# A last attention layer with its norms on ScalarE, and expert products merged to 512 columns

## The chip, the cores and the metric

One NeuronCore of a Trainium2 chip runs the whole program: TensorE (PE) multiplies, VectorE (DVE) and ScalarE (ACT) work on rows in SBUF and PSUM, GpSimd (POOL) on rows in SBUF only and issues indirect DMAs, and SyncE (SP) issues most DMAs. The metric is the device time of one execution in microseconds; lower is better.

## What is computed

Four transformer layers over 32 row blocks of 128 rows and 256 columns. Layers 0 and 1 are cross-attentions with a feed-forward net behind layer 0, layer 2 is a decoder layer (causal attention, cross-attention, then a mixture of 8 experts of which each row takes 2), layer 3 is a windowed attention with a gate, an RMS norm and a centring over each block. The code numbers the attentions 0 to 4, so that "layer 4" there is the last one. The parts which the change touches:

```
router_weights = softmax(xf @ rw + rb);  topw, topi = top_k(router_weights, 2);  topw = softmax(topw)
h   = gelu(xf @ w1[e] + b1[e]);  eo = h @ w2[e] + b2[e]          # for each expert e
x   = layernorm(x + sum over the row's 2 experts of topw * eo)   # ln3
attn = (softmax(q k / 4, window of 128) v) @ Wo + bo             # 16 heads, one key/value head
gate = silu(concat(attn, query) @ Wg + bg)
out  = attn * gate + query * (1 - gate)
x_hat = out * rsqrt(mean(out^2) + 1e-6) * rms_w
y    = x_hat - mean(x_hat over the 128 rows of a block)
```

## The kernel before

Every engine has a program of its own, and semaphores order them. It has three stages.

**Attention stage.** `slots` runs 8 iterations of 16 slots (4 attentions for 4 row blocks) and a tail. In the last attention's slots the router's logits are made; seven slots later `rank` (L956) counts, with a triangular and an all-ones matmul in float32 over `ohm5`, how many rows before each row chose the same expert. DVE turns ranks into positions (`ranks`, `positions`), and POOL scatters each row twice into `sorted_x` (`scatter`, L1949), where every expert has a span of its own; `base` keeps each expert's next free row.

**Hand-over and experts.** After the last ranks DVE makes tables (`tlink`, L1717, one linked step after another): `tails`, from which SP zeroes 128 rows behind each expert's last; the number of tiles of each expert; for each of 71 tiles its address and expert (loop at L1733, three steps an expert); then the positions in the packed result (L1757 to L1760). SP loads tile 0 after all zero fills, scatters and tables (L591 to L606). For each tile PE runs `up` (16 products 128x128, L1071), the transposes of the next tile (L685) and `down` (L1075). For `down` the hidden values and the weights are split into a high and a low part, and high x high, high x low and low x high are summed in `ps_w`, in matmuls of 256 columns (L1084). DVE splits the hidden values (`tile_split`, L1779) and adds the bias to the result (`tile_y`, L1773), POOL splits the weights of expert e while e-1 runs (`split_w2`, L2010), ACT applies gelu and copies the weights of `up`.

**Last layer.** `cslots` runs 32 slots (one for each row block) and a drain. Names with c(d) are the row block d slots ahead. POOL gathers the two expert rows of block c(4) (`gather`, L2036), DVE combines them for c(3) (`combine`, L1826: two products, then the statistics), POOL takes the root (`c_root`), DVE applies the norm for c(2) (`combine_apply`, L1841), POOL makes the residual rows (`c_residual`, L2047). PE runs scores, transposed scores and the products with the values for now and c(-1), then the gate for c(-2) (L1118, L1122); DVE takes the maxima of the scores (`maxima`, L1482), which PE transposes (L877) before the transposed scores, and applies the gate (`gate_open`, `gate_apply`). The RMS norm of c(-3) goes over ACT (`mean_square`), POOL (L2086), DVE (`rms_apply`, L1866), PE (`mean`, L1129) and ACT (`finish`, L1370), which copies the result for the store of c(-4). Before the first slot come constants (L1135 to L1148 on PE, L1809 to L1824 on DVE): products of the biases with weights that let bo, bv and bg be added once.

Each engine carries out its program in the written order; nothing is reordered, so what stands ahead of a waiting operation on its engine, and what behind, can be read from the code.

## Time and profile before

| | us |
|---|---|
| median of 3 runs | 2302.21 |
| lowest, highest | 2299.98, 2303.04 |
| the profiled execution | 2305.83 |
| its span, first to last instruction | 2304.0 |
| attention stage, to about | 1380 |
| experts, from 1407 to about | 1900 |
| last layer, maxima of block 0 and of block 31 | 1923.6, 2276.1 |

The profile is one execution. PE was busy 92% of the span, DVE 71%, ACT 47%, POOL 45%; the granted TensorE clock had a mean of 0.976 of full speed. These shares are means over three stages with different limits. In a timeline row stand the start and duration in microseconds, engine, line, operation, output<-input with the number of operations merged, and in brackets how long the engine had been idle and what ended that. A row of a group has the busy time in microseconds, the mean of one in nanoseconds, and the idle time before.

### The profile page before, as it was taken

Reading aid. Unit: us, or ns where it says so; the run is one execution under the profiler, and the core shown is the slowest. Engines: PE = TensorE matmul, PEld = TensorE weight load, DVE = VectorE, ACT = ScalarE, POOL = GpSimd, SP = SyncE. Lnnn points to the kernel's source line nnn. Section 1 sums busy time; section 2 is a strip of 40 time slices with the busy share of each in tenths; the row PEclk is TensorE's granted clock in tenths of the full one; section 3 lists DMA queues with packets and bytes.
Section 4 is the critical chain, followed back from the end, with each engine's and each line's share of the span. In section 5 each row is a group of like instructions: output and inputs, shape, how many; then the busy total and the mean of one; then the engine's idle time right before and its main releaser. Section 6 shows DMA issues by size and latency. Waiting matters only on the chain.

```text
span 2304.0 us, 84589 instructions
## 1 busy us (share of the span) xinstructions
PE 2108.5 (92%) x31768; PEld 1837.1 (80%) x31769; DVE 1644.6 (71%) x3373; ACT 1092.9 (47%) x2804; POOL 1038.3 (45%) x1304
## 2 busy tenths in 40 slices
PE   5999999999999999999999975999999997888897
PEld 4877877878878878878878755999999996676776
DVE  4688787787787887887887875444544446889986
ACT  2345344354454344453444433556555553555554
POOL 3445455455455454554554634110211007767763
PEclk9999999999999999999999987999999997999989
DMA  8401001001001001001000103121221112211110
GB/s 196 163 3 38 8 21 43 7 19 42 9 19 39 11 19 36 16 19 31 18 22 4 39 29 133 50 64 39 60 70 39 39 32 82 59 55 56 56 50 21
DMA packets 93477, 101.02 MB, mean 44 GB/s; under 512 B 23968, under 2 KB 84384, under 8 KB 93088
## 3 DMA queue, kind: packets, MB, share of 16 engines
q1 hardware_dynamic: 84128, 72.02, 10.4%
q0 software_dynamic: 8704, 25.19, 3.5%
q8 instruction: 203, 3.33, 0.6%
q14 instruction: 58, 0.48, 0.1%
q10 hardware_dynamic: 384, 0.01, 0.0%
HBM read 64.94 MB, written 32.24 MB: 42 GB/s over the span
## 4 chain that ended last, share of the span: by engine, by line
PE 56%; issue 17%; DVE 15%; ACT 5%; POOL 4%; DVEq 1%; SPq 1%; DMA 1%; POOLq 0%; ACTq 0%
PE ps_scores L1071 10%; PE ps_w L1084 9%; PE ps_o L897 8%; PE ps_scores L858 4%; ACT pt_all L1242 4%; PE ps_qk L779 4%; PE ps_qk L745 4%; DVE rs L1492 3%; PE ps_xv L685 2%; PE ps_xv L763 2%; DVE lower L1473 2%; PE ps_scores L805 1%; PE ps_scores L865 1%; PE ps_w L944 1%; POOL rstd L1940 1%
## 5 line engine op out<-in xcount | busy, mean ns | idle before, releaser
L1485 DVE TENSOR_REDUCE mb<-ps_scores 128x16 bf16<-128x2048 f32 x160 | 365.8, 2286 | 57.8 <-PE ps_scores L838 54.2
L1492 DVE RECIPROCAL rs<-ps_o 128x256 f32<-128x256 f32 x160 | 280.4, 1752 | 33.1 <-PE ps_o L897 29.0
L1242 ACT ACTIVATE pt_all<-ps_scores 128x512 f32<-128x512 f32 x512 | 263.5, 602 | 48.4 <-PE ps_scores L865 48.4
L1071 PE MATMUL ps_scores<-tiles,w_now 128*128 128x128 f32 x2272 | 267.4, 276 | 1.2 <-DVE tiles L1767 1.2
L1071 PEld LDWEIGHTS ps_scores<-tiles,w_now 128*128 128x128 f32 x2272 | 262.0, 193 | 1.8 <-issue 1.8
L1328 ACT ACTIVATE tiles<-ps_scores,b1s 128x128 f32<-128x128 f32 x568 | 154.2, 383 | 204.6 <-PE ps_scores L1071 178.8
L1940 POOL TENSOR_TENSOR rstd<-ve,neghalf 128x1 f32<-128x1 f32 x192 | 109.6, 571 | 308.0 <-DVE ve L1503 268.1
L1084 PE MATMUL ps_w<-w_split,g_split 128*128 x1704 | 224.3, 288 | 7.5 <-DVE g_split L1787 5.8
L1924 POOL TENSOR_TENSOR lower<-lower,consts 128x512 fp32r<-128x512 f32 x160 | 171.3, 1071 | 123.7 <-DVE lower L1473 77.5
L1084 PEld LDWEIGHTS ps_w<-w_split,g_split 128*128 128x128 f32 x1704 | 210.0, 192 | 12.4 <-issue 9.5
L1917 POOL TENSOR_TENSOR qbd_all<-qT,consts 128x512 fp32r<-128x512 f32 x160 | 167.3, 1046 | 104.9 <-ACT kT L1228 74.4
L897 PE MATMUL ps_o<-pt_all,vz 128*32 128x128 f32 x5120 | 176.4, 277 | 2.3 <-issue 2.3
L897 PE MATMUL ps_o<-pt_all,onz 128*32 128x128 f32 x5120 | 171.2, 273 | 0.0
L1777 DVE TENSOR_TENSOR tiles<-ps_w,tiles 128x256 f32<-128x256 f32 x71 | 30.2, 425 | 193.6 <-PE ps_w L1084 193.6
L897 PEld LDWEIGHTS ps_o<-pt_all,vz 128*32 128x32 f32 x5120 | 131.7, 110 | 26.3 <-issue 17.6
L1320 ACT COPY w_now<-w_experts 128x2048 f32 x72 | 140.1, 1948 | 25.1 <-DVE pos_all L1760 25.1
L1945 POOL TENSOR_TENSOR xr<-xn,arena 128x256 f32<-128x256 f32 x128 | 93.1, 727 | 124.1 <-DVE xn L1507 124.1
L1213 ACT ACTIVATE xT<-ps_xv,cols_all 128x128 f32<-128x128 f32 x256 | 103.2, 453 | 90.1 <-PE ps_xv L685 87.0
L897 PEld LDWEIGHTS ps_o<-pt_all,onz 128*32 128x32 f32 x5120 | 144.6, 110 | 0.2
L2018 POOL CAST w_split<-w_raw 128x512 fp32r<-128x512 f32 x32 | 18.2, 609 | 276.8 <-DVE g_split L1787 271.5
L1231 ACT ACTIVATE qT<-ps_qk,cols_all 128x128 fp32r<-128x128 f32 x192 | 60.4, 369 | 173.2 <-PE ps_qk L779 173.2
L2041 POOL DMA_INDIRECT arena<-sorted_y,pidx x64 | 63.2, 987 | 173.5 <-ACT pidx L1354 158.5
(247 smaller groups left out, 4830.2 us busy)
## 6 DMA issues: line engine op xcount, KB each, us to landing
tiles<-sorted_x SPq DMA_DIRECT2D x72, 128.0 KB, 2.0
sorted_y<-tiles SPq DMA_DIRECT2D x71, 128.0 KB, 1.7
w_experts<-in_L_xattn_e_w SPq DMA_DIRECT2D x8, 1024.0 KB, 10.4
w_raw<-in_L_xattn_e_w POOLq DMA_DIRECT2D x8, 1024.0 KB
ct_scratch<-cT SPq DMA_DIRECT2D x32, 128.0 KB, 1.7
x_scratch<-x2b_all SPq DMA_DIRECT2D x32, 128.0 KB, 1.7
arena<-x_scratch SPq DMA_DIRECT2D x32, 128.0 KB
cT<-ct_scratch SPq DMA_DIRECT2D x32, 128.0 KB, 2.1
```

The costliest lines, as they stand in the source:

```text
L897: last = mm(ps_o[32 * q:32 * q + 32, 2 * kind + c, :], w, pt[:, SLOTS * q + PAIR * c + par, :], start=par == 0, stop=par == 1, tile_positi ...
L1071: last = mm(ps_s[:, 2 * par + j // 4, P * (j % 4):P * (j % 4 + 1)], w1_now[:, par, c, P * j:P * (j + 1)], xgT[par][:, c, :], start=c == 0, ...
L1084: last = mm(ps_w[:, 0:D], g_split[:, g_, j, :].bitcast(F32R), w2_split[:, bass.ds(odd * (2 * FC * D) + (w_ * FC + j) * D, D)].bitcast(F32R ...
L1213: last = nc.scalar.activation(xT[n["s"]][:, c, :], src[:, c, :], ACT.Identity, bias=col[b_][:, c:c + 1], scale=col[g][:, c:c + 1])
L1242: nc.scalar.activation(pt[:, 4 * g:4 * g + 4, :].rearrange("p h q -> p (h q)"), ps_s[:, g, :], ACT.Exp, bias=bias, scale=LAYER[l]["scale"] ...
L1320: nc.scalar.copy(w1_now[:, par].rearrange("p c n -> p (c n)"), w1f[:, bass.ds(e * (KC * FF), KC * FF)]).then_inc(w1_copied, 1)
L1328: last = nc.scalar.activation(gT[:, j, :], ps_s[:, 2 * par + j // 4, P * (j % 4):P * (j % 4 + 1)], ACT.Gelu, bias=b1s[par][:, j:j + 1])
L1485: V.tensor_reduce(mb[:].rearrange("p (g r) -> p g r", g=BANKS)[:, :, 0:SLOTS], ps_s[:].rearrange("p g (h k) -> p g h k", h=SLOTS), AX_X, A ...
L1492: V.reciprocal(rs[:], ps_o[:, 2:4, :]).then_inc(recip_ready, 1)
L1917: G.tensor_tensor(qbd[p].bitcast(F32R), qT[:].unsqueeze(2).to_broadcast([P, KC, PAIR, P]), hmask.unsqueeze(1).unsqueeze(3).to_broadcast([P ...
L1924: G.tensor_tensor(qbd_lo.bitcast(F32R), qT_lo.unsqueeze(2).to_broadcast([P, KC, PAIR, P]), hmask.unsqueeze(1).unsqueeze(3).to_broadcast([P ...
L1940: G.tensor_tensor(rstd[kind][:], ve[kind][:], neghalf[:], ALU.pow).then_inc(done, 1)
```

## The change

It has four parts.

1. *Last layer.* The combination's norm is applied by ACT, as yb x rstd + c_nb with c_nb = -mean x rstd from POOL, and the RMS scaling by ACT too; the RMS weight moves behind the centring, into DVE's `finish`, which reads PSUM and replaces ACT's copy. `finish` stands ahead of the maxima. DVE's combination of c(3) and gate of c(-2) are written in turns instead of one after the other. On POOL the gather moves to the end of the slot, the low part of the queries (`expand_lo`) from the end to its beginning.
2. *Constants ahead.* The bias products of the last layer are made on PE and DVE while the experts' first tile is awaited; so is the window mask. The first slot's work is reordered: keys and values before the transposes, scores of block 0 before the projections of block 1.
3. *Hand-over to the experts.* The per-tile tables are made for all 8 experts in one operation each (`past`, `steps`, 128x568), 12 linked steps instead of 41. The tails are zeroed half an iteration earlier, 640 rows for each expert instead of 128. The update of the positions comes after the copies of tiles 0 and 1. The ranks are counted in bfloat16.
4. *Experts.* High and low weights lie side by side, so that the high hidden part multiplies both in one matmul of 512 columns; the sum of the two halves is a second DVE operation in `tile_y`. `tile_split` has one cast and one subtraction of 1024 columns instead of two each of 512. POOL's split has 8 casts of 256 and 16 subtractions of 128 columns instead of 4 of 512 and 8 of 256.

```diff
@@ rank (PE)
-            mm(ps_w[:, D:D + (NS + 1) * E], tri, ohm5[:].rearrange("p s e -> p (s e)"), start=True, stop=False)
+            mm(ps_w[:, D:D + (NS + 1) * E], tri_b, ohm5[:].rearrange("p s e -> p (s e)"), start=True, stop=False)
@@ SP, in the last iteration's slots; POOL waits for tail_zeroed before its last scatters
+            if last and tau == TPI // 2:
+                sp.wait_ge(consts_ready, 1)
+                sp.wait_ge(tails_ready, 1)
+                for e in range(E):
+                    r = sp.value_load(tails[0:1, e:e + 1], min_val=0, max_val=DUMMY - TAIL)
+                    sp.dma_start(sorted_x[bass.ds(r, TAIL), :].rearrange("(a p) d -> p a d", p=P),
+                                 zeros[:].unsqueeze(1).to_broadcast([P, TAIL // P, D])).then_inc(tail_zeroed, 16)
@@ tables (DVE)
-        for e in range(E):
-            tlink(V.tensor_scalar(tb[:, 4], tile_iota, incl[:, e:e + 1], None, ALU.is_ge))
-            tlink(V.tensor_tensor(eid, eid, tb[:, 4], ALU.add))
-            tlink(V.scalar_tensor_tensor(ex_, tb[:, 4], n_t[:, e:e + 1], ex_, ALU.mult, ALU.add))
...
+        tlink(V.tensor_tensor(past[:], tile_iota.unsqueeze(2).to_broadcast([P, TILES, E]), by_tile(incl), ALU.is_ge))
+        tlink(V.tensor_tensor(steps[:], past[:], by_tile(shift[:]), ALU.mult))
+        V.tensor_reduce(eid, past[:], AX_X, ALU.add)
+        tlink(V.tensor_reduce(row_, steps[:], AX_X, ALU.add))
@@ down (PE)
+            def part(g_, j):
+                n = 2 * D if g_ == 0 else D
+                return mm(ps_w[:, 0:n], g_split[:, g_, j, :].bitcast(F32R),
+                          w2_split[:, bass.ds(odd * (2 * FC * D) + j * 2 * D, n)].bitcast(F32R),
+                          start=j == 0 and g_ == 0, stop=j == FC - 1 and g_ == 0)
@@ tile_y (DVE)
-            V.tensor_tensor(ys[par], ps_w[:, 0:D], b2.rearrange("p e d -> p (e d)")[:, bass.ds(e * D, D)], ALU.add).then_inc(b_y, 1)
+            V.tensor_tensor(ys[par], ps_w[:, 0:D], b2.rearrange("p e d -> p (e d)")[:, bass.ds(e * D, D)], ALU.add).then_inc(b_part, 1)
+            wait_apart(dve, b_part, k + 1)
+            V.tensor_tensor(ys[par], ps_w[:, D:2 * D], ys[par], ALU.add).then_inc(b_y, 1)
@@ last layer (ACT), combine_apply before mean_square, rms_apply after xt_evac
+            nc.scalar.activation(xn[n["s"]][:], yb[n["p"]][:], ACT.Identity, bias=c_nb[:], scale=rstd[2][:]).then_inc(c_xn, 1)
...
+            nc.scalar.activation(xh[n["p"]], go, ACT.Identity, bias=0.0, scale=rstd[3][:]).then_inc(c_xh, 1)
@@ c_root (POOL)
+            root(2, c_ln, COMBINE * b + 5, c_root_done)
+            wait(pool, c_root_done, b + 1)
+            G.tensor_tensor(c_nb[:], c_nm[:], rstd[2][:], ALU.mult).then_inc(c_rstd, 1)
@@ finish (DVE), ahead of maxima
+            wait(dve, c_mean, b + 1)
+            wait(dve, c_at, last_at)
+            wait(dve, c_out[n["p"]], 16 * n["h"])
+            V.tensor_tensor(fin[n["p"]], ps_w[:, D:2 * D], row3["L3_xattn_rms_w"][:], ALU.mult).then_inc(c_fin, 1)
```

Of the moved instructions three places are shown, each first before, then after. Numbers of lines are those of the file they stand in. First PE, one tile's down product: address loads and its first matmuls.

```order
L1078 ISA x2
L98 REGISTER_ALU
L1084 ISA
L1084 MATMUL ps_w<-w_split,g_split 128x256
L1084 ISA
L1084 MATMUL ps_w<-w_split,g_split 128x256 x2
```

```order
L1110 ISA x2
L99 REGISTER_ALU
L1116 ISA
L1116 MATMUL ps_w<-w_split,g_split 128x512
L1116 MATMUL ps_w<-w_split,g_split 128x256
```

Of three matmuls of 256 columns for each of the 8 blocks, one of 512 and one of 256 are left. Next DVE, one slot of the last layer from behind the maxima (the gate is L1855, L1861, L1863, L1864 before and L1888, L1893, L1898, L1902 after; the combination is L1831 to L1839 and L1865 to L1884).

```order
L1845 TENSOR_SCALAR xn<-yb,mv,rstd 128x256
L1492 RECIPROCAL rs<-ps_o 128x256
L1494 TENSOR_TENSOR oT<-ps_o,rs 128x256
L1855 TENSOR_TENSOR arena<-ps_w,row_L_xattn_bg 128x256
L1869 SCALAR_TENSOR_TENSOR arena<-arena,rstd,row_L_xattn_rms_w 128x256
L1831 SCALAR_TENSOR_TENSOR arena<-arena,w_all 128x256
L1833 SCALAR_TENSOR_TENSOR yb<-arena,w_all 128x256
L1835 BN_STATS st_2<-yb 128x6
L1837 BN_AGGR mv<-st_2 128x2
L1839 TENSOR_SCALAR ve<-mv 128x1
L1861 SCALAR_TENSOR_TENSOR arena<-arena 128x256
L1863 SCALAR_TENSOR_TENSOR arena<-arena 128x256
```

```order
L1532 RECIPROCAL rs<-ps_o 128x256
L1534 TENSOR_TENSOR oT<-ps_o,rs 128x256
L1888 TENSOR_TENSOR arena<-ps_w,row_L_xattn_bg 128x256
L1865 SCALAR_TENSOR_TENSOR arena<-arena,w_all 128x256
L1893 SCALAR_TENSOR_TENSOR arena<-arena 128x256
L1871 SCALAR_TENSOR_TENSOR yb<-arena,w_all 128x256
L1898 SCALAR_TENSOR_TENSOR arena<-arena 128x256
L1875 BN_STATS st_2<-yb 128x6
L1902 TENSOR_TENSOR arena<-arena,xr 128x256
L1880 BN_AGGR mv<-st_2 128x2
L1883 TENSOR_SCALAR c_nm<-mv 128x1
L1884 TENSOR_SCALAR ve<-mv 128x1
```

The norm and the RMS scaling are gone from DVE, and each operation now has one of the other chain between it and its predecessor. Last POOL, one slot of the last layer (L2041 and L2093 are the gathers).

```order
L1940 TENSOR_TENSOR rstd<-ve,neghalf 128x1
L1917 TENSOR_TENSOR qbd_all<-qT,consts 128x512
L2041 DMA arena<-sorted_y,pidx 128x256 x2
L2086 TENSOR_TENSOR rstd<-ve,neghalf 128x1
L2059 TENSOR_TENSOR arena<-arena 128x256
L2051 TENSOR_TENSOR xr<-xn,row_L_xattn_ln_g 128x256
L2053 TENSOR_TENSOR arena<-xr,arena 128x256
L2054 TENSOR_TENSOR xr<-xr,row_L_xattn_ln_b 128x256
L1924 TENSOR_TENSOR lower<-lower,consts 128x512
```

```order
L1990 TENSOR_TENSOR rstd<-ve,neghalf 128x1
L2102 TENSOR_TENSOR c_nb<-c_nm,rstd 128x1
L1974 TENSOR_TENSOR lower<-lower,consts 128x512
L1967 TENSOR_TENSOR qbd_all<-qT,consts 128x512
L2144 TENSOR_TENSOR rstd<-ve,neghalf 128x1
L2108 TENSOR_TENSOR xr<-xn,row_L_xattn_ln_g 128x256
L2110 TENSOR_TENSOR arena<-xr,arena 128x256
L2111 TENSOR_TENSOR xr<-xr,row_L_xattn_ln_b 128x256
L2116 TENSOR_TENSOR arena<-arena 128x256
L2093 DMA arena<-sorted_y,pidx 128x256 x2
```

The low part of the queries moved from the end to the third place, the gathers to the end, the difference (L2059, L2116) behind the residual rows, and c_nb is new.

## Rows read from the trace of the kernel before

**Rows 1.** Busy time of each engine in three stretches, with TensorE's granted clock.

```profile
1300.00:1450.00 150.00, 107.63 (x1551) 95.63 (x1552) 98.96 (x239) 59.29 (x136) 61.94 (x80) 0.84 0.23 78
1600.00:1700.00 100.00, 98.34 (x842) 97.07 (x841) 47.12 (x102) 57.00 (x133) 19.94 (x26) 1.00 0.19 59
2000.00:2100.00 100.00, 86.80 (x1568) 71.19 (x1569) 88.12 (x142) 52.12 (x158) 70.58 (x87) 0.95 0.19 55
```

**Rows 2.** All instructions of line 1485: number, min/median/max ns, first and last start.

```profile
L1485 DVE TENSOR_REDUCE mb<-ps_scores x32: 2291/2292/2293, 1923.6 to 2276.1; 128x16 bf16<-128x2048 f32 x32
```

**Rows 3.** Timeline, start and duration: two maxima that follow each other near the end.

```profile
2257.08 2.29 DVE L1485 TENSOR_REDUCE mb<-ps_scores 128x16 bf16<-128x2048 f32 x1
2267.26 2.29 DVE L1485 TENSOR_REDUCE mb<-ps_scores 128x16 bf16<-128x2048 f32 x1 [1.42 <-PE ps_scores L838]
```

**Rows 4.** Groups by line and shape, 1950 to 2280: busy us, mean ns, idle.

```profile
L1831 DVE SCALAR_TENSOR_TENSOR arena<-arena,w_all 128x256 f32<-128x256 f32 x26 | 26.1, 1004 | 0.0
L1869 DVE SCALAR_TENSOR_TENSOR arena<-arena,rstd,row_L_xattn_rms_w 128x256 f32<-128x256 f32 x28 | 23.2, 830 | 3.4
L1864 DVE TENSOR_TENSOR arena<-arena,xr 128x256 f32<-128x256 f32 x29 | 19.4, 668 | 1.0
L1845 DVE TENSOR_SCALAR xn<-yb,mv,rstd 128x256 f32<-128x256 f32 x27 | 11.7, 435 | 0.0
L1855 DVE TENSOR_TENSOR arena<-ps_w,row_L_xattn_bg 128x256 f32<-128x256 f32 x28 | 11.6, 415 | 0.0
L1940 POOL TENSOR_TENSOR rstd<-ve,neghalf 128x1 f32<-128x1 f32 x27 | 18.0, 666 | 37.0 <-DVE ve L1839 36.9
```

**Rows 5.** Timeline: the same VectorE product beside two different GpSimd operations.

```profile
1910.56 0.96 POOL L2041 DMA_INDIRECT arena<-sorted_y,pidx  x1 [0.30 <-issue]
1910.95 0.48 DVE L1831 SCALAR_TENSOR_TENSOR arena<-arena,w_all 128x256 f32<-128x256 f32 x1 [5.09 <-DMA arena<-sorted_y,pidx]
...
2065.30 1.22 POOL L1924 TENSOR_TENSOR lower<-lower,consts 128x512 fp32r<-128x512 f32 x1
2065.55 1.26 DVE L1831 SCALAR_TENSOR_TENSOR arena<-arena,w_all 128x256 f32<-128x256 f32 x1
```

**Rows 6.** Chain that ended last: an expert tile, and four of line 910's.

```profile
1481.49 3.57 PE ps_scores L1071 x32
1485.28 2.96 PE ps_w L1084 x24
...
1984.85 0.86 PE ps_w L910 x4
```

**Rows 7.** Timeline of the experts, DVE casts without and beside GpSimd's split.

```profile
1605.40 0.75 DVE L1784 CAST g_split<-tiles 128x512 fp32r<-128x512 f32 x2
1612.24 1.50 DVE L1784 CAST g_split<-tiles 128x512 fp32r<-128x512 f32 x2
```

**Rows 8.** Timeline of the hand-over to the experts.

```profile
1378.02 1.85 PE L962 MATMUL ps_w<-route_all,one_f 128*128 128x32 f32 x8
...
1390.21 0.96 POOL L1953 DMA_INDIRECT sorted_x<-x2b_all,posu  x1 [0.30 <-issue]
...
1393.01 5.98 DVE L1741 TENSOR_SCALAR tbi<-xT 128x71 int32<-128x71 f32 x1
...
1401.06 0.36 SPq L600 DMA_DIRECT2D tiles<-sorted_x  x1
1401.09 0.26 DVE L1759 TENSOR_SCALAR yb<-yb,shift 128x64 f32<-128x64 f32 x1
```

**Rows 9.** Timeline of the hand-over to the last layer.

```profile
1899.96 0.42 DVE L1777 TENSOR_TENSOR tiles<-ps_w,tiles 128x256 f32<-128x256 f32 x1 [5.01 <-PE ps_w L1084]
...
1905.61 0.29 ACT L1354 CAST pidx<-pos_all 128x2 uint32<-128x2 f32 x2 [13.99 <-DVE row_L_xattn_bg L1821]
1906.68 1.03 POOL L2041 DMA_INDIRECT arena<-sorted_y,pidx  x1 [158.46 <-ACT pidx L1354]
```

**Rows 10.** The page's DMA issues: KB each, median us from issue to landing.

```profile
sorted_y<-tiles SPq DMA_DIRECT2D x71, 128.0 KB, 1.7
```

328 lines of the change are left out of this document (176 added, 152 removed).

## The prediction

> **What bounds the kernel now.** I read the busy time by stretch first; it tells three regimes apart [rows 1]: among the experts (1600 to 1700) TensorE (PE) is busy 98.3 of 100 us and VectorE (DVE) 47; in the last layer (2000 to 2100) DVE has 88.1, PE 86.8 at a granted clock of 0.95; the stretch of the hand-over to the experts (1300 to 1450) has gaps on all engines, and a clock of 0.84. So a microsecond taken from PE among the experts counts in full, one taken from DVE in the last layer counts until PE is the bound, and in between the chain decides.
>
> The last layer's maxima (L1485) run 32 times, from 1923.6 to 2276.1 [rows 2]: 352.5 us over 31 steps, 11.37 us a slot. What a slot costs when DVE is not late is seen near the end, where gathers and combination have run out: from 2257.08 to 2267.26, 10.18 us, and there DVE waited 1.42 us for PE [rows 3]. That is the floor which PE sets; 1.19 us a slot lies above it.
>
> **The last layer.** Part of that excess is DVE work that lasts longer than it needs. The first combination product (L1831) has a mean of 1004 ns, the RMS scaling (L1869) 830, the gate's sum (L1864) 668, though a like one on 128x256 that reads PSUM takes 415 (L1855) [rows 4]. The timeline shows with whom they collide: L1831 lasts 1.26 us beside GpSimd's (POOL's) L1924, but 0.48 beside POOL's gather L2041 [rows 5]. The change removes from DVE the normalisation L1845 (0.435) and the RMS scaling (0.830), adds the weighted finish (like L1855, 0.415) and one tiny scaling c_nm (taken at 0.15), and puts the gather last on POOL, where the combination and gate operations of DVE run beside it. With L1831 at its undisturbed 0.48 and L1864 at the 0.42 of L1855, DVE loses 0.435 + 0.830 + 0.52 + 0.25 - 0.415 - 0.15 = 1.47 us of work a slot. It had 88.1/100 x 11.37 = 10.0, so about 8.5 remain. That is under the floor of 10.18: PE sets the slot. Writing the two chains in turns also hides their waits on each other; I don't add that, as DVE has slack already.
>
> The norm's new price is latency. The bias c_nb is one more POOL operation of 128x1, at most the 666 ns of L1940 [rows 4], and the application on ScalarE (ACT) waits for it with mean square and maxima copy queued behind. ACT is busy 52 of 100 us [rows 1] and has room for two more operations of the size of L1855. POOL, with 70.6 per 100 us (8.0 a slot) plus at most 0.7, stays under 10. On DVE the finish now stands ahead of the maxima, waits for ACT's copy of the attention rows, and PE's next transposes wait for those maxima. In the undisturbed slot nothing stood there, so I charge its issue step, 0.3 us of the 0.415, in full: a slot of 10.45 instead of 11.37 us (the last two, short already, lengthen a little: that is inside the rounding). 31 x 0.92 = **28.5 us**. Bounds: 10.2 gives 36, 11.0 gives 11.
>
> The Trainium skill, "SBUF — State Buffer", who interferes with whom, calls the pair of ports that VectorE and GpSimd share an exclusive lock, taken by a VectorE operation with two SBUF inputs against GpSimd operations that read SBUF, the second fully blocked. The pair of L1831 rows agrees. By that rule the new order would save what I count, and the casts in the expert stage, which may take both ports, would block in the same way; that is the rival on the other side below.
>
> **The experts.** Each of the 71 tiles has 24 matmuls of 256 columns, 2.96 us, after 3.57 us of up projections (L1071) [rows 6]: 2.96/24 = 0.123 us each. The change makes them 8 of 512 and 8 of 256 columns; the columns streamed are the same, 8 of 24 starts go. If all cost lies in the columns, the gain is zero. If a 256-column one costs 0.123 and a 512-column one its stream alone, take L910: its four instructions of one 128x256 product in float32, at two passes, need 0.86 us, 0.215 each [rows 6], and that is the same stream as 512 columns at one pass. Then 8 x (0.215 + 0.123) = 2.70, 0.26 less. I take 0.18, between this and a fixed cost for each start (0.123 less 256/512 of 0.215 is 0.016, of which eight go: 0.13). 71 x 0.18 = 12.8 us, bounds 0 and 18.
>
> Against it stands a longer DVE chain before each down product: the tile's sum becomes two operations (0.42 each), while two casts and two subtractions become one each. I reckon 0.6 us more, which the 3.57 us of up projection still hide. Where POOL splits the next expert's weights the cover is gone: two casts (L1784) take 1.50 instead of 0.75 us [rows 7]. POOL's split now has 24 short operations instead of 12, so it lasts longer, perhaps 2 tiles instead of 1 for each of 6 experts; at 0.4 us for each of 12 tiles: minus 5 us. Net **8 us**, bounds -5 and 18.
>
> The Trainium skill, "TensorE: Matmul & The Clock Gate", back-to-back issue gap, gives N/2.4 + 2.5 ns, 109 ns at 256 columns. The row says 123, so here it doesn't hold as it stands; by it the merge would save only 8 x 2.5 ns a tile, 1.4 us in all, which is the second rival.
>
> **The hand-over to the experts.** Before, the ranks' float32 matmuls (L960, L962; the last takes 1.85 us from 1378.02), then 41 linked table steps on DVE, one of which, L1741, lasted 5.98 us beside POOL's split; tile 0 is loaded at 1401.06. The last scatter starts at 1390.21 and takes 0.96 us [rows 8]. After, the ranks are in bfloat16 (1.5 us earlier) and the table has 12 steps; from about 1380, at even 0.6 us each, it ends by 1388. So the scatter is late next: 1391.17 - 1.5 + its landing, for which I take a tile store's 1.7 us [rows 10] = 1391.4. The load comes 9.7 us earlier. SyncE (SP) has given its zero fills off by then: they are issued half an iteration before, five times as long (8 x 640 rows), and only POOL's last scatters wait for them. Given back: the 15 position updates of 0.26 us (L1759) now stand between tile 1's copy and tile 0's split, 4 us of which ACT's gelu covers about half: 2 us. Net **8 us**, bounds 4 and 10. In the seven earlier iterations the ranks' ten matmuls lie on PE's queue at full clock; half precision and half the passes save perhaps 0.4 us each, **3 us**, bounds 0 and 7.
>
> **The hand-over to the last layer.** ACT's index copy started at 1905.61, after waiting 13.99 us for the constants (L1821) [rows 9]. With the constants made ahead, the gather waits only for the last tile's store: that can be issued from 1900.4 on, when DVE's last sum ends [rows 9], lands 1.7 us later [rows 10], and comes 1 us later for the longer chain: with some 0.3 us of issue 1903.4, against 1906.7 for the gather [rows 9]. **3 us**, bounds 0 and 5; the earlier scores of row block 0 are swallowed by the third block's combination, which stands ahead of its maxima.
>
> **The sum.** 28.5 + 8 + 8 + 3 + 3 = 50.5 us. The profiled execution took 2305.83 us, 1.83 outside its span, and is 3.6 above the median of 2302.21. So 2255.3 by its own time, and 2251.7 by the median: 2252.
>
> **Rivals.**
> *The slot stays with DVE or POOL.* POOL's residual operations and the difference now come together before the gather; if they reach into DVE's five operations with two SBUF inputs, each may go to 1.26 us as L1831 did. Two of five add 1.6 us to 8.5 and give 10.1, three 10.9. Slot 11.0: 28.5 becomes 11.5, total 33.5, 2269. For it: DVE's 88% and POOL's 71%; against it: the 0.48 beside the gather.
> *The merge saves nothing on PE* (all cost in the columns, or 2.5 ns a start) while the longer split costs 5 us: experts +4 instead of -8, 2264. For it: no row has a 512-column full-array product. Both together: 2281.
> *Slower than before: the single cast starves.* L1741 waited through the whole of POOL's split. If the one cast of 1024 columns, or the subtraction behind it, does so each time, PE waits for about the split's length, some 12 us, six times: 72 us against 50.5, 2324. It decides from 8.4 us an expert. Against it: today's casts only double beside the same operations [rows 7], and they get in between.
> *The change doesn't act*: the slot was never DVE's. Then the 1.42 us wait for PE in the undisturbed slot would stand in all slots; it stands only where the work is gone [rows 3], so this has next to no weight.
>
> **How the numbers follow.** Forecast 0.52, slot rival 0.20, merge rival 0.15, both 0.07, slower 0.04, near nothing 0.02. The forecast's own bounds run from 2232 (slot at the floor, merge at its best) to 2262; the range goes on over the two single rivals to 2276 and leaves out the double and the slow one. Faster by more than 0.2% (4.6 us, about what a measurement of this kernel can tell from no change): 0.93; within it: 0.02; slower: 0.05.
>
> **What would show it.** Right: the maxima 10.2 to 10.7 us apart with DVE waiting for PE's scores, the combination product near 0.48 us, tiles 6.5 to 6.6 us apart, the first tile load near 1388 (3 us of the ranks included), the first gather 3 us after the last store's issue. Wrong: combination or gate operations still above 0.8 us, PE waiting for maxima or for the ScalarE norm, down products still 2.9 us, PE stalls of several us wherever POOL splits weights, or a granted clock well under 0.95 in the last layer.

## The result, and the profile after

The changed kernel took 2282.89 us in the median of five executions (2274.13 to 2288.45), the kernel before 2302.21 (2299.98 to 2306.12): a ratio of 0.990, with a 95% interval of 0.988 to 0.992. It is faster, by 19 us; 50 were forecast, and 2282.89 lies above the range of 2232 to 2276.

By stages, from one profile each (the changed kernel's is of its fastest execution, 2274.13 us; the last column is another execution of the same file, on another chip, and belongs to the experiments):

| | forecast | measured | the same file on a second chip |
|---|---|---|---|
| to the first tile's sum (hand-over, ranks) | -11 | -10.5 | -9.7 |
| first to last tile's sum | -8 | -14.8 | -14.8 |
| last tile's sum to the first maxima | -3 | -3.3 | -3.4 |
| 31 slots of the last layer | -28.5 | -2.4 | -38.8 |
| drain | 0 | -0.7 | -0.7 |
| span | -50.5 | -31.7 | -67.4 |

The first sum is DVE's L1777 or L1820 of tile 0. The two spans differ by more than the two medians, 31.7 against 19.3 us: the profiled execution of before is 3.6 us above its median, that of the changed kernel 8.8 below. Two terms are near, the experts gave more, and the last layer gave next to nothing. The maxima of the last layer, which answer [rows 2], first in the changed kernel:

```profile
L1525 DVE TENSOR_REDUCE mb<-ps_scores x32: 2280/2281/2293, 1895.0 to 2245.1; 128x16 bf16<-128x2048 f32 x32
```

350.1 us over 31 steps, 11.29 a slot (before: 11.37), most of them 11.6. Busy time by stretch, as [rows 1]:

```profile
1300.00:1450.00 150.00, 120.64 (x1577) 104.58 (x1571) 94.91 (x221) 66.38 (x154) 68.61 (x104) 0.89 0.23 75
1600.00:1700.00 100.00, 100.00 (x754) 94.23 (x755) 49.37 (x92) 60.12 (x138) 24.17 (x51) 1.00 0.20 60
2000.00:2100.00 100.00, 86.27 (x1619) 70.07 (x1622) 72.54 (x150) 58.74 (x174) 74.46 (x96) 1.00 0.19 58
```

In the last layer DVE fell from 88.1 to 72.5 of 100 us, 8.4 us in a slot of 11.6, where 8.5 were forecast. But PE didn't become busier: no engine is full. The groups by form (as [rows 4]) show the operations as quick as hoped:

```profile
L1865 DVE SCALAR_TENSOR_TENSOR arena<-arena,w_all 128x256 f32<-128x256 f32 x22 | 10.5, 476 | 0.0
L1902 DVE TENSOR_TENSOR arena<-arena,xr 128x256 f32<-128x256 f32 x22 | 9.0, 407 | 0.0
L1910 DVE TENSOR_TENSOR arena<-ps_w,row_L_xattn_rms_w 128x256 f32<-128x256 f32 x22 | 9.3, 425 | 58.1 <-ACT arena L1427 31.2 <-issue 25.7 <-PE ps_w L1169 1.3
```

The freed time is now idle time ahead of L1910, the weighted finish: 58.1 us in 22 slots. The timeline of one slot says what it waits for:

```profile
2048.04 0.40 PE L882 MATMUL ps_scores<-mT,ecol_b 32*128 32x128 bf16 x16
2048.12 1.24 POOL L2093 DMA_INDIRECT arena<-sorted_y,pidx  x1 [0.16 <-issue]
2048.24 0.41 ACT L1447 ACTIVATE arena<-arena 128x256 f32<-128x256 f32 x1
2049.66 1.13 POOL L2093 DMA_INDIRECT arena<-sorted_y,pidx  x1 [0.30 <-issue]
2051.06 2.06 ACT L1269 ACTIVATE pt_all<-ps_scores 128x512 f32<-128x512 f32 x4 [2.41 <-remote]
2053.24 0.43 ACT L1427 COPY arena<-ps_w 128x256 f32<-128x256 f32 x1
2053.81 0.42 DVE L1910 TENSOR_TENSOR arena<-ps_w,row_L_xattn_rms_w 128x256 f32<-128x256 f32 x1 [2.83 <-ACT arena L1427]
2054.15 2.28 DVE L1525 TENSOR_REDUCE mb<-ps_scores 128x16 bf16<-128x2048 f32 x1
```

L882 ends the transposed scores at 2048.44 and signals it; the exponentials (L1269) wait for nothing else. In the attention stage they start 0.43 us behind L882's start; here 3.0 us, and the profile can't name the releaser ("remote"). Behind them stand ACT's copy of the attention rows (L1427), DVE's finish and maxima, PE's transposes, the next L882: a ring. The lateness is 3.0, 2.2 or 1.5 us in the 24 slots that hold gathers from the fifth on, most often 3.0, and 0.4 to 0.6 in the last four, where there is no gather. In the kernel before the gathers end 1.5 us or more ahead of that signal, and the exponentials start 0.4 to 0.9 us behind its L865, the same operation.

### The profile page after: what moved, and what is told of

Same layout as the page of the kernel before. It is cut to its first block, busy times and chain, and to the rows that moved or that the text cites. A ratio compares the mean times of both kernels' runs of the same rounds, so it can differ in the third digit from the quotient of the medians.

```text
span 2272.3 us, 82689 instructions
## 1 busy us (share of the span) xinstructions
PE 2078.6 (91%) x31160; PEld 1786.5 (79%) x31161; DVE 1583.1 (70%) x3281; ACT 1110.7 (49%) x2836; POOL 1063.6 (47%) x1432
## 4 chain that ended last, share of the span: by engine, by line
PE 58%; issue 17%; DVE 11%; ACT 6%; POOL 5%; another core or an unknown queue 1%; DMA 1%; SPq 1%; DVEq 0%; ACTq 0%; POOLq 0%
PE ps_scores L1103 11%; PE ps_w L1116 9%; PE ps_o L914 8%; PE ps_scores L875 5%; ACT pt_all L1269 5%; PE ps_qk L796 4%; PE ps_qk L762 4%; DVE mb L1525 3%; PE ps_xv L702 3%; PE ps_xv L780 2%; DVE lower L1513 2%; PE ps_scores L822 2%; PE ps_scores L882 2%; PE ps_w L961 1%
## 5 line engine op out<-in xcount | busy, mean ns | idle before, releaser
L1269 ACT ACTIVATE pt_all<-ps_scores 128x512 f32<-128x512 f32 x512 | 264.6, 603 | 102.7 <-remote 51.5
L1103 PEld LDWEIGHTS ps_scores<-tiles,w_now 128*128 128x128 f32 x2272 | 266.9, 193 | 4.9 <-issue 1.8
L1116 PE MATMUL ps_w<-w_split,g_split 128*128 x1136 | 217.0, 343 | 5.7 <-DVE g_split L1829 5.7
L1116 PEld LDWEIGHTS ps_w<-w_split,g_split 128*128 128x128 f32 x1136 | 173.1, 188 | 30.2 <-issue 6.5
L1820 DVE TENSOR_TENSOR tiles<-ps_w,tiles 128x256 f32<-128x256 f32 x71 | 30.2, 425 | 184.7 <-PE ps_w L1116 184.7
L2093 POOL DMA_INDIRECT arena<-sorted_y,pidx x64 | 73.4, 1147 | 163.3 <-DMA sorted_y<-tiles 147.9
L2071 POOL CAST w_split<-w_raw 128x256 fp32r<-128x256 f32 x64 | 24.2, 424 | 243.8 <-DVE g_split L1829 238.4
```

Of the source, the lines that this page charges most:

```text
L1103: last = mm(ps_s[:, 2 * par + j // 4, P * (j % 4):P * (j % 4 + 1)], w1_now[:, par, c, P * j:P * (j + 1)], xgT[par][:, c, :], start=c == 0, ...
L1116: return mm(ps_w[:, 0:n], g_split[:, g_, j, :].bitcast(F32R), w2_split[:, bass.ds(odd * (2 * FC * D) + j * 2 * D, n)].bitcast(F32R), start ...
L1269: nc.scalar.activation(pt[:, 4 * g:4 * g + 4, :].rearrange("p h q -> p (h q)"), ps_s[:, g, :], ACT.Exp, bias=bias, scale=LAYER[l]["scale"] ...
```

## Experiments

Each call ran on one chip with the kernel before beside it. What they found, since it takes the runs together:

| kernel | chip | exponentials behind L882, us | slot, us | median, us | ratio to before |
|---|---|---|---|---|---|
| changed | a | 1.5 to 3.0 | 11.29 | 2282.9 | 0.990 |
| gathers in mid-slot | b | 0.5 to 1.0 | 10.99 | 2269.5 | 0.984 |
| no turns | b | 1.5 to 3.0 | 10.80 | 2257.9 | 0.979 |
| before, gathers late | b | 0.7 | 11.01 | 2291.2 | 0.995 |
| gathers behind an exponential | c | 0.5 | 10.12 | 2237.3 | 0.974 |
| plain loads | c | 0.5 | 10.23 | 2234.1 | 0.971 |
| two-input cast | c | 0.5 | 10.12 | 2266.5 | 0.985 |
| unmerged | c | 0.5 | 10.13 | 2242.7 | 0.975 |
| changed, again | d | 1.5 to 3.0 | 10.82 | 2268.6 | 0.986 |
| gathers behind, again | d | 0.5 | 10.66 | 2268.4 | 0.985 |
| cast on ScalarE | d | 0.5 | 10.54 | 2263.4 | 0.982 |
| changed, third time | e | 0.5 | 10.12 | 2241.8 | 0.976 |
| one signal | e | 0.5 | 10.11 | 2244.5 | 0.977 |
| gathers in the window | e | 0.5 | 10.12 | 2245.1 | 0.977 |
| one signal, again | f | 1.5 to 3.0 | 11.17 | 2273.9 | 0.989 |
| gathers in the window, again | f | 0.5 | 10.21 | 2244.9 | 0.976 |

The slot is (last start - first start)/31 of the maxima; intervals of the ratios are 0.002 to 0.004 to either side. Medians are of three to five executions, those of no turns and plain loads of two. The kernel before had 2298 to 2304 us on all of them. Each chip was used in one call, so where the text says chip, the call can't be told from it.

### The gathers' place

*In mid-slot*, on POOL:

```diff
             if nxt["ok"]:
                 expand(nxt)
+            if c(4)["ok"]:
+                gather(c(4))
...
-            if c(4)["ok"]:
-                gather(c(4))
```

> The changed kernel with one move: on GpSimd (POOL) the two gathers of the last layer stand again where they stood before, behind the expansion of the next queries and ahead of the RMS root, instead of at the slot's end. In the changed kernel the slot is 11.6 us, ScalarE (ACT) stands idle 2.4 us before the exponentials although the last product of the transposed scores (L882) started 3.0 us earlier, and it starts 0.27 us after the second gather has ended; in the four slots without a gather it starts 0.4 to 0.6 us after L882. Theory G (the gather beside VectorE's run of combination and gate holds up TensorE's signals): here the exponentials start 0.4 to 0.9 us behind L882, the idle 2.4 us are gone, the slot is 10.0 to 10.5 us, the execution about 2245 to 2255 us. Rival N (the gather is a bystander; the wait comes with the new orders of ACT or VectorE): the idle 2.4 us stay, slot 11.6, 2283 us. Rival P (POOL gets late): the wait is gone, but the RMS root or the residual rows come 2 us later and the slot stays above 11 us.

The exponentials start 0.5 to 1.0 us behind L882: as theory G has it. But the slot is 10.99, not 10.5 or less (one slot of 14.35, at half the clock for 10 us, makes 0.1 of it). Now POOL's residual rows and difference lie beside the combination, and both engines suffer, which is the prediction's first rival:

```profile
L1871 DVE SCALAR_TENSOR_TENSOR yb<-arena,w_all 128x256 f32<-128x256 f32 x26 | 22.0, 845 | 0.8
L1865 DVE SCALAR_TENSOR_TENSOR arena<-arena,w_all 128x256 f32<-128x256 f32 x26 | 16.2, 622 | 0.0
L1898 DVE SCALAR_TENSOR_TENSOR arena<-arena 128x256 f32<-128x256 f32 x27 | 12.2, 452 | 30.6 <-POOL arena L2116 30.5
```

0.845 and 0.622 us instead of 0.485 and 0.476, and 1.1 us a slot of waiting for POOL's difference.

*No turns*: the combination whole, ahead of `gate_silu`, `gate_product` and `gate_sum`; the gathers stay last.

```diff
+                for part in (combine_first, combine_second, combine_stats, combine_moments):
+                    part(c(3))
+            if g_["ok"]:
+                for part in (gate_silu, gate_product, gate_sum):
+                    part(g_)
```

> The changed kernel with VectorE's combination of c(3) written as a whole ahead of the gate's last three operations (as before the change), instead of in turns with them; the gather stays at the slot's end. Theory G in its narrow form (the gather is held up by, or holds up, any run of VectorE operations on SBUF): VectorE's run is as long as now, so the exponentials stay 2 to 3 us late and the slot is 11.6 us or, with the waits between linked operations back, up to 12; 2283 to 2300 us. Rival N2 (the density of the turns, an operation every 0.3 us, does it): the 2.4 us shrink to below 1 and the slot falls to 10.3 to 10.8 us, about 2255 us.

The lateness stays, with more of its shorter steps: 2.2 us on average, slot 10.80. The narrow form of theory G holds as to the lateness; its 11.6 us and 2283 us do not. Slot and time (10.80 us, 2257.9 us) are near those of rival N2, but its reason is missing, as the lateness didn't shrink to below 1 us. Whether the turns make the steps longer is open: the changed kernel in turns had 10.82 on chip d.

*Before, gathers late*: the same move made in the kernel before.

```diff
-            if c(4)["ok"]:
-                gather(c(4))
...
                 expand_lo(nxt)
+            if c(4)["ok"]:
+                gather(c(4))
```

> The kernel before with one move: the gathers of the last layer stand at the end of POOL's slot, behind the expansion of the low part, as after the change. Theory G (place alone): the exponentials, which start 0.7 to 0.9 us behind the last product of the transposed scores in the kernel before, start later wherever a gather lies behind that product, and the slot grows above its 11.37 us; or, since here POOL's residual rows and the low part stand ahead of it, the gather falls behind the exponentials and beside VectorE's gate, and nothing is late but VectorE's L1831 is quicker (0.48 instead of 1.0 us): slot 11.0 to 11.4. Rival N: no idle time before the exponentials in any case, and the time within 5 us of 2302.

The gathers fall 2.3 us behind L865, after the exponentials have begun, and nothing is late: 12 us faster. It isn't L1831, whose mean is now 1.26 us; the gate's sum L1864 has 0.426 instead of 0.668 [rows 4], and the slots are 11.1 to 11.6 where they varied from 10.7 to 14.3.

*Behind an exponential*:

```diff
             if c(4)["ok"]:
+                wait(pool, probs_ready, 4 * now["t"] + 1)
                 gather(c(4))
```

> The changed kernel with one wait more: at the slot's end POOL starts the two gathers only when the first exponential of the slot is done. So far: gathers behind L882 by 0.1 to 2.8 us, exponentials 1.5, 2.2 or 3.0 us behind L882, slot 11.3 us; gathers ahead of L882 (the kernel with them in mid-slot), exponentials 0.5 to 1.0 us behind, slot 10.9 us. Theory G (a gather that runs while TensorE signals the ends of L882 holds those signals up, in steps of 0.75 us): here no gather runs then, the exponentials start 0.4 to 0.9 us behind L882 in every slot, DVE keeps its quick combination, and the slot is 10.0 to 10.4 us; execution 2240 to 2255 us. Rival P (POOL late): the gathers end 1.2 us later, the next root of the norm waits for them, and ScalarE's norm, the transposes and the slot follow: 10.8 to 11.2 us, 2262 to 2272 us. Rival N: the lateness stays, 11.3 us.

*Plain loads* on SyncE in place of POOL's gathers (other rows, same bytes):

> The changed kernel with the two gathers of each block replaced by two plain loads of 128 rows each from the same tensor, issued by SyncE behind the load of the residual rows, with the same waits for the indices and the combination; the rows are then not those of the routing, so the output differs. POOL issues nothing in the last layer; the same bytes land at about the same moment. Theory G (it is POOL's issuing instruction): exponentials 0.4 to 0.9 us behind L882, slot 10.0 to 10.4 us, about 2245 us. Rival D (it is the transfers themselves): the exponentials still start 1.5 to 3 us behind L882, slot above 11, about 2275 us.

Both have 0.5 us and slots of 10.1 (plain loads: 10.23, with one slot of 14.4 in which the granted clock was 0.63 and PE's matmuls took up to twice as long). That looked like proof. It wasn't: the next two kernels in the same call, whose last layer is that of the changed kernel, have it as well.

### The chip

The two-input cast and the unmerged products (below) change only the expert stage. Their gathers stand from 0.1 to 1.3 and from 1.6 to 2.8 us behind L882, where the changed kernel has them; their slots are 10.12 and 10.13. So the changed kernel itself was run again, twice.

> The changed kernel itself, unchanged, beside two others on one chip. So far its profile and that of the kernel without turns have exponentials 1.5 to 3.0 us behind L882 while a gather runs; two others with the gathers at the same place to 0.1 us (the two-input cast, the unmerged products: both differ from the changed kernel in the expert stage alone) have them 0.51 us behind and slots of 10.12 us. Those that were late and those that were not ran on different chips. Theory K (the lateness beside a gather belongs to the chip or the execution, not to the code): on a chip of the second kind this kernel has slots of 10.1 us and takes about 2240 to 2250 us; on one of the first kind 11.3 us and about 2280. Rival A (it belongs to the code, by the place of instructions or the phase at which the last layer begins): here, on whichever chip, slots of 11.3 us and 2275 to 2288 us again.

> The changed kernel itself, as the control for the two others of this call. Where the chip holds up TensorE's signals beside a gather: exponentials 1.5 to 3.0 us behind L882, slots of 10.8 to 11.3 us, 2264 to 2288 us. Where it does not: 0.5 us behind, slots of 10.1 us, 2232 to 2245 us. In either case a cast that starved (one in the last profile, 5.7 us instead of 0.68) costs some 8 us for each.

On chip d it is late and takes 2268.6, on chip e it isn't and takes 2241.8 us. The same slot, on chip e:

```profile
2052.63 0.40 PE L882 MATMUL ps_scores<-mT,ecol_b 32*128 32x128 bf16 x16
2052.74 1.21 POOL L2093 DMA_INDIRECT arena<-sorted_y,pidx  x1 [0.17 <-issue]
2052.83 0.41 ACT L1447 ACTIVATE arena<-arena 128x256 f32<-128x256 f32 x1
2053.14 2.05 ACT L1269 ACTIVATE pt_all<-ps_scores 128x512 f32<-128x512 f32 x4
2054.26 1.12 POOL L2093 DMA_INDIRECT arena<-sorted_y,pidx  x1 [0.30 <-issue]
```

To L1269 each distance is that of chip a within 0.04 us; the exponentials then come at 0.51 instead of 3.02. Theory K holds, for the chip or the call. Of the five chips b to f three show the lateness and two don't; a, on which the change was measured, shows it too and may be one of the three. On chip e the busy times from 2000 to 2100 are those of the forecast, PE the bound:

```profile
2000.00:2100.00 100.00, 98.10 (x1869) 80.44 (x1870) 83.73 (x169) 66.80 (x200) 84.67 (x111) 1.00 0.22 66
```

The traces hold a control for this that is the same in every kernel. In the last iteration of the attention stage one scatter of POOL, also an indirect DMA, is issued 0.3 us behind the start of the transposed scores, so that it meets their signal. First the kernel before the change, then the changed kernel on chip e:

```profile
1288.33 0.41 PE L865 MATMUL ps_scores<-mT,ecol_b 32*128 32x128 bf16 x16
1288.62 1.07 POOL L1953 DMA_INDIRECT sorted_x<-x2b_all,posu  x1 [0.17 <-issue]
1289.19 2.06 ACT L1242 ACTIVATE pt_all<-ps_scores 128x512 f32<-128x512 f32 x4 [0.95 <-PE ps_scores L865]
```

```profile
1289.18 0.41 PE L882 MATMUL ps_scores<-mT,ecol_b 32*128 32x128 bf16 x16
1289.48 1.07 POOL L2003 DMA_INDIRECT sorted_x<-x2b_all,posu  x1 [0.17 <-issue]
1289.67 2.06 ACT L1269 ACTIVATE pt_all<-ps_scores 128x512 f32<-128x512 f32 x4 [0.58 <-PE ps_scores L882]
```

The exponentials start 0.86 us behind in the one and 0.49 in the other. In all 17 profiles this place has 0.86 to 0.91 us on the chips with the lateness (b, d, f, and a with the profile of before) and 0.46 to 0.49 on the others (c, e), whatever the kernel. So the difference belongs neither to the changed kernel nor to its last layer, and the profile of before had it.

### What is held up

*Behind an exponential, again*, on chip d beside the changed kernel:

> The changed kernel with the gathers waiting for the first exponential of the slot, on the same chip as the changed kernel itself. Theory G and K together (the lateness needs both a chip that shows it and a gather that runs while TensorE signals): slots of 10.1 us here on any chip, 2236 to 2248 us, however late the changed kernel is. If the wait does nothing and the chip all: as the changed kernel of this call, within 3 us. If the changed kernel has 11.3 us slots here, the difference should be 31 x 1.18 = 36 us.

The exponentials are on time, yet the slot is 10.7 against 10.1 on chip c, and the time is that of the changed kernel on this chip (2268.4 and 2268.6 us). Each of the two profiles has one starved cast of the expert stage (below). The same kernel, the same place, first chip c, then d:

```profile
2065.24 0.95 POOL L2093 DMA_INDIRECT arena<-sorted_y,pidx  x1 [0.30 <-issue]
2065.59 0.40 PE L855 MATMUL ps_scores<-kT,qbd_all 32*128 32x128 bf16 x16
2065.93 0.42 DVE L1910 TENSOR_TENSOR arena<-ps_w,row_L_xattn_rms_w 128x256 f32<-128x256 f32 x1 [0.97 <-issue]
2066.27 2.28 DVE L1525 TENSOR_REDUCE mb<-ps_scores 128x16 bf16<-128x2048 f32 x1
```

```profile
2063.35 0.96 POOL L2093 DMA_INDIRECT arena<-sorted_y,pidx  x1 [0.30 <-issue]
2063.70 0.40 PE L855 MATMUL ps_scores<-kT,qbd_all 32*128 32x128 bf16 x16
2064.04 0.42 DVE L1910 TENSOR_TENSOR arena<-ps_w,row_L_xattn_rms_w 128x256 f32<-128x256 f32 x1 [1.24 <-issue]
2065.03 2.29 DVE L1525 TENSOR_REDUCE mb<-ps_scores 128x16 bf16<-128x2048 f32 x1 [0.56 <-PE ps_scores L855]
```

Now PE's signal of the next scores (L855) meets the second gather, and the maxima start 0.65 us late, 1.33 behind L855 instead of 0.68. So it isn't ACT or the exponentials alone that suffer: both late operations wait for a signal of PE that is sent while a gather is issued. DVE's wait for ACT in the same time (L1893 behind L1447) and PE's own matmuls go on. In the second and third slot on chip a the profile shows it on PE itself: the last matmuls of L882, which carry the signals, stand apart, in the second slot by 0.64 and 0.74 us:

```profile
1912.30 0.94 POOL L2093 DMA_INDIRECT arena<-sorted_y,pidx  x1 [0.30 <-issue]
1912.36 0.29 PE L882 MATMUL ps_scores<-mT,ecol_b 32*128 32x128 bf16 x8
1913.00 0.27 PE L882 MATMUL ps_scores<-mT,ecol_b 32*128 32x128 bf16 x4 [0.35 <-issue]
1913.74 0.27 PE L882 MATMUL ps_scores<-mT,ecol_b 32*128 32x128 bf16 x4 [0.48 <-issue]
```

The steps of 0.74 us suggested one for each signal. *One signal* for the four banks tests that:

```diff
-                    if u == SLOTS - 1:
-                        last.then_inc(st_ready, 1)
+                    if u == SLOTS - 1 and (l != 4 or g == BANKS - 1):
+                        last.then_inc(st_ready, 4 if l == 4 else 1)
```

> The changed kernel with the end of the transposed scores signalled once, by the last of its matmuls and for all four banks, instead of by four matmuls, one for each bank. Theory Q (each signal of TensorE takes one step of 0.74 us while a gather is issued, and four of them make the 2.2 to 3.0 us): the exponentials start 0.5 to 1.5 us behind L882, mean about 1.0, the slot is 10.1 to 10.5 us, 20 to 30 us less than the control. Rival W (nothing gets through until the gather ends, however many signals): still 1.5 to 3.0 us behind, within 4 us of the control. On a chip without the lateness: as the control within 3 us.

> The kernel with one signal in place of four again. If its gathers hold nothing up (exponentials 0.5 us behind L882, slots of 10.12 us) the chip is of the quiet kind and the run tells nothing. On a chip of the other kind: theory Q (a step of 0.74 us for each signal of TensorE): exponentials 0.5 to 1.5 us behind L882, slot 10.1 to 10.5 us. Rival W (nothing gets through until the gather ends): 1.5 to 3.0 us behind, slot 10.8 to 11.3 us, as the changed kernel on the chips on which it was late.

Chip e was without lateness and told nothing. On chip f, with a quarter of the signals, the exponentials are 1.5, 2.2 or 3.0 us behind all the same, slot 11.17: a step for each signal falls. Rival W's numbers came, its reason only in part: the gathers are issued from 0.1 to 1.3 and from 1.6 to 2.8 us, and a release at 2.2 us lies within the second.

*In the window*: the gathers go between PE's urgent signals.

```diff
             wait_apart(pool, c_ln, COMBINE * (b - 2) + 2)
+            if signalled is not None:
+                wait_apart(pool, st_ready, signalled)
...
-                gather(c(4))
+                gather(c(4), 4 * now["t"] + 4)
```

> The changed kernel with the gathers held until the transposed scores are signalled for all four banks (and with that wait as the last ahead of them), so that they are issued from 0.3 to 2.7 us behind the signal, while ScalarE does the exponentials and TensorE the next projections; the kernel that waited for the first exponential issued its second gather from 9.00 to 9.96 us of the slot, when TensorE signals the next scores at 9.75, and the maxima started 0.66 us late on the chip that shows the lateness (slot 10.7 us) and not on the other (10.1). Theory G (signals that coincide with a gather are all of it): 10.0 to 10.2 us a slot on any chip, exponentials 0.5 to 0.9 us behind L882; on a chip with the lateness 15 to 18 us less than the 2268 us of the kernel that waited for the exponential, 2240 to 2255 us. Rival F (the signals of values, queries and mean, which fall into this window, are held up too and matter): slot 10.5 us or more on such a chip.

> The kernel with the gathers held until the end of the transposed scores is signalled. On the quiet chip they were issued from 1.3 to 3.8 us behind L882, 0.8 us behind the first exponential. On a chip of the other kind: theory G: the signals of values, queries and mean fall into that time but have 1.0 us or more to spare, the next urgent one (the attention rows' product) comes at 3.0 us or later and may be caught: 10.1 us a slot if not, 10.5 if it is; the kernel whose gathers came 0.9 us later had 10.7. Rival F (it matters little where they stand): 10.7 us or more.

On chip f, beside the kernel with one signal that is late there:

```profile
2041.38 0.40 PE L882 MATMUL ps_scores<-mT,ecol_b 32*128 32x128 bf16 x16
2041.88 2.05 ACT L1269 ACTIVATE pt_all<-ps_scores 128x512 f32<-128x512 f32 x4
2042.70 1.19 POOL L2095 DMA_INDIRECT arena<-sorted_y,pidx  x1 [1.36 <-PE ps_scores L882]
2044.19 0.96 POOL L2095 DMA_INDIRECT arena<-sorted_y,pidx  x1 [0.30 <-issue]
```

10.21 us a slot (five slots of 10.5, most others 10.0 or 10.1) and 2244.9 us, 29 less than its neighbour. On chip e it costs nothing measurable: 2245.1 against the changed kernel's 2241.8, ranges 2239 to 2249 and 2238 to 2243. On a chip with the lateness it is the fastest version measured, 2.4% faster than the kernel before; on a quiet one it can't be told from the changed kernel.

### The experts

In the profile of the mid-slot kernel, whose expert stage is the changed kernel's, two of 71 casts starve, that is, they don't end before POOL's run of subtractions does; one of them:

```profile
1480.24 6.65 POOL L2075 TENSOR_TENSOR w_split<-w_raw,w_split 128x128 fp32r<-128x128 f32 x16
1481.95 5.49 DVE L1827 CAST g_split<-tiles 128x1024 fp32r<-128x1024 f32 x1
1487.60 1.23 DVE L1829 TENSOR_TENSOR g_split<-tiles,g_split 128x1024 fp32r<-128x1024 f32 x1 [0.15 <-DVE g_split L1827]
1489.03 1.43 PE L1116 MATMUL ps_w<-w_split,g_split 128*128 x3 [4.46 <-issue]
```

The cast holds from 1481.95 to 1487.44, 0.55 us past the end of POOL's sixteen subtractions, and PE stands 4.46 us. Mostly the cast gets in (0.7 to 1.0 us), and then POOL's run lasts 8.15 us instead of 6.65. In 13 profiles with this cast, each with six splits of an expert's weights beside the tiles, it starved four times. First to last sum: 464.2 us in the changed kernel on chips a and e, without a starved cast; 473.0 twice with one, 480.6 with two. Of that 7 to 8 us belong to each (its tile takes 13.7 to 13.9 us instead of 6.6, and the next one up to 7.3), the rest to a lower clock in the last tile. That is the prediction's slow rival, at about one in twenty splits instead of every one. It may be a part of spreads such as the changed kernel's 2274 to 2288 us, whose profile, with none, is the fastest; in which of its executions casts starved isn't recorded.

The Trainium skill, "SBUF — State Buffer", who interferes with whom, says that whoever issues first gets the shared ports and the other fully blocks, and counts copies and casts among the operations that can take both. The row agrees that a one-input cast is kept out altogether. But it is kept out for sixteen operations of POOL, not for one.

```diff
-            V.tensor_copy(g_split[:, 0].bitcast(F32R), gT).then_inc(b_high, 1)
+            V.tensor_tensor(g_split[:, 0].bitcast(F32R), gT, gT, ALU.max).then_inc(b_high, 1)
```

> The changed kernel with the cast of the hidden values (L1827, one input, 0.683 us undisturbed) written as a maximum of the tile with itself, which gives the same values from an operation with two inputs like the subtraction behind it (L1829), which lasted 1.226 us and never over 1.245 in any profile. In the profile of the kernel with the gathers in mid-slot, which has the same expert stage, two of the casts lasted 5.49 and 5.75 us, to the end of POOL's subtractions, and TensorE stood 4.5 us after each; in that of the changed kernel none did. Theory S (these starved casts, none to several in an execution, are why the changed kernel's times spread over 14 us and its median lies above its best): here no execution has one, the times lie within 5 us of each other and the median is near the changed kernel's best, 2274 to 2280 us (the chain is 0.54 us longer, which the up projection still hides or nearly). Rival L (the longer chain reaches TensorE): down products start late in all 71 tiles, by 0.1 to 0.4 us, 2282 to 2305 us. Rival E (the spread comes from elsewhere): times still spread over 10 us or more.

```profile
L1827 DVE TENSOR_TENSOR g_split<-tiles x71: 1212/1215/1422, 1407.3 to 1896.1; 128x1024 fp32r<-128x1024 f32 x71
```

None starves, longest 1.42 us, and the four executions lie within 7 us (2262.3 to 2269.6); the changed kernel's four on chip e lie within 4. But rival L came too: 6.97 us a tile (mean of tiles 10 to 60) instead of 6.64. Of the 0.53 us added 0.33 reached PE, so the slack of the chain was some 0.2 us.

*Cast on ScalarE* behind gelu, waiting for the down product; VectorE only subtracts. The gathers wait for an exponential here too, so the kernel to compare with is the one with the gathers behind, on the same chip.

```diff
             last.then_inc(b_gelu, 1)
+            wait(act, b_gelu, k + 1)
+            wait(act, b_down, k)
+            nc.scalar.copy(g_split[:, 0].bitcast(F32R), gT).then_inc(b_high, 1)
```

> As the run before, and the cast of the hidden values (0.683 us on VectorE, or 5.5 us where it starves beside POOL's split) moved to ScalarE, behind gelu, where it waits for the last tile's down product; VectorE only subtracts. ScalarE was busy 60 of 100 us among the experts, 4.0 of 6.63 us a tile, and the copy of 1024 columns should take half of the weight copy's 1.95 us. Theory S (starved casts make the spread of 10 to 14 us): the executions lie within 5 us, tiles 6.63 us apart everywhere, median 2230 to 2237 us. Rival T (ScalarE becomes late: its copy of the next weights stands behind a wait for the down product): up projections start late, tiles 6.8 to 7.2 us apart, 2250 to 2275 us.

The mean is 7.03 us a tile, which is rival T's number, but not for its reason. It comes from five tiles of 9.7 to 11.3 us where POOL splits; the others keep 6.63 us, as in the changed kernel, so ScalarE with its copy of 1.05 us isn't late. In those five it is the subtraction, an operation with two inputs, that starves. One of them:

```profile
1510.06 6.67 POOL L2076 TENSOR_TENSOR w_split<-w_raw,w_split 128x128 fp32r<-128x128 f32 x16
1511.37 1.05 ACT L1360 CAST g_split<-tiles 128x1024 fp32r<-128x1024 f32 x1 [0.89 <-PE ps_w L1116]
1512.52 5.29 DVE L1830 TENSOR_TENSOR g_split<-tiles,g_split 128x1024 fp32r<-128x1024 f32 x1
```

It takes 5.28 to 5.35 us instead of 1.22 in five of the six splits, where the cast of the changed kernel starved in about one of twenty. So two inputs are no protection, and why the maximum on VectorE, 1.42 us at most, and the subtraction right behind it got in, stays open. The executions spread over 12 us (2257.9 to 2269.6), the profiled one being the slowest; how many starved in the others isn't recorded.

*Unmerged*: seven of eight 512-column products split again.

```diff
-                for g_ in (0, 1) if j < FC - 1 else (1, 0):
-                    last = part(g_, j)
+                for g_, lo in ((0, 0), (0, D), (1, 0)) if j < FC - 1 else ((1, 0), (0, 0), (0, D)):
+                    last = part(g_, j, lo, D)
```

> The changed kernel with the products of the high hidden part split again for seven of the eight blocks: two matmuls of 256 columns in place of one of 512, into the same two halves; all else stays. Theory M (each start costs: a tile's down product goes from 2.97 to 2.89 us by eight starts less): down product about 2.96 us again, tiles 6.70 us apart instead of 6.63, 71 x 0.07 = 5 to 7 us more. Rival C (cost lies in the columns, and the shorter tile came from somewhere else): tiles 6.63 apart, no difference. By the prediction's 0.18 us a tile it would be 11 us.

A tile takes 6.70 us instead of 6.64 (mean of tiles 10 to 60). Two down products each from the chains of waits, of the changed kernel and of this one:

```profile
1480.31 2.94 PE ps_w L1116 x16
...
1487.05 2.93 PE ps_w L1116 x16
```

```profile
1481.17 3.02 PE ps_w L1115 x23
...
1487.98 2.96 PE ps_w L1115 x23
```

Theory M: each start costs 0.060/7 = 9 ns; all eight make 0.069 us a tile, 4.9 us in 71.

## Why the prediction was wrong, point by point

**The ranks and the first hand-over** (11): right in sum, with the parts displaced. The maxima of the last attention slot come 0.6 us earlier in the profile on chip a and 1.3 us later in that on chip e, so of the 3 us for the ranks in earlier iterations nothing shows (the last ones gave 2.0 where 1.5 were forecast). The table ends at 1383.1 and the last scatter begins at 1386.99; the scatter is late next, as forecast. Tile 0 is loaded 10.8 us earlier, and only 0.3 us were given back.

```profile
1386.99 0.96 POOL L2003 DMA_INDIRECT sorted_x<-x2b_all,posu  x1 [0.30 <-issue]
1390.30 1.44 SPq L620 DMA_DIRECT2D tiles<-sorted_x  x2
```

The load stands 2.35 us behind the scatter's end; I had taken 1.7 from a plain store [rows 10].

**The experts** (8, measured 14.8): the merge is 4.9 us where 12.8 were forecast, too high by far, since I chose a value between the float32 row and the fixed cost of a start. That fixed cost, worked out there as 16 ns, measured 9. The 1.4 us for the stage by the rule of the Trainium skill, "TensorE: Matmul & The Clock Gate", back-to-back issue gap, are too low. The term with the wrong sign is the split, whose longer run was to cost 5 us. The six tiles of the kernel before that took 7.6 to 7.8 us instead of 6.8, PE waiting beside POOL's split, are gone: some 6 us. A single cast that gets in lasts 0.8 to 1.0 us, where [rows 7] has two in 1.50. The last tile took 6.40 us instead of 7.31, since its down product ran at full clock (3.05 us, granted clock 1.00) and not at 0.63 as before (4.64 us). That 0.9 us is luck: eight of twelve profiles of this expert stage have 4.4 to 5.5 us there. Some 3 us of the 14.8, in the ordinary tiles, have no name.

**The second hand-over** (3): 3.3. The first gather came at 1878.08, 3.0 us behind the end of the last tile's first sum, as reckoned, but split otherwise: 0.5 us for the second sum (1.0 reckoned) and 2.6 for the store (2.0).

**The last layer** (28.5): the step that failed. DVE's work is right to 0.1 us, PE as the bound is right, and 10.45 us was even too careful: where nothing is held up the slot is 10.12, 38.8 us for the layer, and the file takes 2241.8 us against the forecast 2252. What failed is the sentence that put the gather last on POOL and saw in it only what runs beside DVE. It stands beside PE's signal of the transposed scores too, and on the chip of the measurement that signal arrives up to 2.5 us late. The time that DVE gave up went into that wait. In the last layer of the profile of before nothing showed it, as its gathers lie where nobody waits for PE; in its attention stage one scatter did, by 0.4 us. None of the rivals had it; the nearest by number, the slot at 11.0, came from DVE and POOL. Whether the forecast's range was met hung on the chip as well: the same file took 2282.9 us on a, 2268.6 on d and 2241.8 on e.

**The slow rival** ("the single cast starves") I gave 0.04. It is real, rare, and cost nothing in the profile shown. It had named the subtraction too, and that is what starved in five of six splits once the cast had left VectorE.

## What to carry to other kernels

An operation moved to a quieter place on its own engine has new neighbours on every other one: go through the signals that are sent while it runs and ask who has no slack for each. A VectorE operation beside a long run of GpSimd operations is a lottery, a cast (5.7 us instead of 0.68) as well as a subtraction of two inputs (5.3 instead of 1.22); look at the longest of its durations, not the mean. And before a cause is called shown, run the unchanged kernel in the same call: two kernels that "cured" the lateness had only met another chip. A place where the same two operations meet in every kernel, as the scatter does here, is a control that costs no run.
